# Two selective scans: the rounding helper of softplus moves from ScalarE to GpSimd, scan inputs are shared out anew, and the preparation of the next chunk is reordered

## The reference, cut to what matters

```python
# layer 1 (first scan): 128 channels d, 64 states n, positions l = 4096 in each of 4 images
u = layernorm(x @ W_in[:, :128]) * gamma + beta
dt, B_ssm, C_ssm = split(u @ W_dt + b_dt, [8, 64, 64])
delta = softplus(dt @ W_dtr + b_dtr)
h[l] = exp(delta[l] * A) * h[l-1] + delta[l] * B_ssm[l] * u[l]      # for each d, n
y = sum_n(h * C_ssm) + u * D + xc * silu(xc)                        # xc: 3x3 depthwise convolution
out = x + y @ W_out
# layer 3 (second scan): the same recurrence with 256 channels, 16 states, over all 16384
# positions, once forwards and once backwards; both results are added and group-normalised
```

## Time and profile before

| | us |
|---|---|
| median of 3 runs | 10018.97 (10010.94 to 10019.53) |
| the profiled execution, its time | 10018.13 |
| the profiled execution, its span | 10016.3 |
| busy in the span: PE, DVE, ACT, POOL | 9175.6, 7849.4, 7926.6, 5764.0 |
| first scan's scans, from the first to the end of the last | 2837.3 to 5734.1 |
| second scan's scans | 6802.0 to 9929.3 |

### The profile page before, as it was taken

How to read it: one execution, slowest core, us unless ns; L and a number is a source line. 1 busy time by engine, 2 the same in 40 slices (tenths; PEclk the granted TensorE clock), 3 DMA queues, 4 the chain that set the end, 5 groups by cost and what they waited for, 6 DMA issues and landing times. The chain is left out here.

```text
span 10016.3 us, 147659 instructions
## 1 busy us (share of the span) xinstructions
PE 9175.6 (92%) x51972; PEld 4789.2 (48%) x51972; DVE 7849.4 (78%) x5926; ACT 7926.6 (79%) x14573; POOL 5764.0 (58%) x3092
## 2 busy tenths in 40 slices
PE   9999999999978888888888899998999999999995
PEld 6767767767733333333333344443333333333332
DVE  7858858858669999999999911117999999999997
ACT  5646646646578998999989855559999999999996
POOL 0000000000068998999989800008999999999996
PEclk9999999999989999999999999999999999999998
DMA  0000000000045555556556500005666666666666
GB/s 40 0 1 0 0 1 0 0 1 0 0 135 185 193 193 183 191 189 195 190 185 194 177 8 8 8 20 171 206 209 203 211 205 211 211 208 212 206 209 232
DMA packets 338546, 1249.85 MB, mean 125 GB/s; under 512 B 39280, under 2 KB 39408, under 8 KB 334448
## 3 DMA queue, kind: packets, MB, share of 16 engines
q1 hardware_dynamic: 338032, 1243.13, 38.2%
HBM read 1144.41 MB, written 56.62 MB: 120 GB/s over the span
## 5 line engine op out<-in xcount | busy, mean ns | idle before, releaser
L2066 DVE TENSOR_TENSOR_SCAN l_h<-l_ring,l_h,l_ps 128x1024 f32<-128x1024 f32 x960 | 2201.5, 2334 | 112.4 <-PE l_ps L1626 87.2
L1024 POOL TENSOR_TENSOR l_hc<-l_h,l_hc 128x1024 f32<-128x1024 f32 x1024 | 2027.0, 2000 | 223.6 <-DVE l_h L1131 201.1
L1989 POOL TENSOR_TENSOR l_ring<-l_h,l_ring 128x1024 f32<-128x1024 f32 x1024 | 2026.3, 2002 | 136.3 <-DVE l_h L2066 130.6
L1131 DVE TENSOR_TENSOR_SCAN l_h<-l_decay,l_h,l_ps 128x1024 f32<-128x1024 f32 x768 | 1747.7, 2330 | 82.1 <-PE l_ps L717 76.0
L117 POOL COPY l_qm<-l_q 128x128 f32 x128 | 82.9, 650 | 2576.2 <-PE l_ps L189 2180.1
L900 ACT ACTIVATE l_xt<-l_duT,l_BT 128x128 f32<-128x128 f32 x4224 | 1286.6, 389 | 113.7 <-PE l_ps L717 112.7
L1856 ACT ACTIVATE l_xt<-l_duT,l_BT 128x128 f32<-128x128 f32 x3840 | 1171.4, 393 | 16.4 <-PE l_ps L1626 15.2
L1643 PE MATMUL l_ps<-l_ring,w_sb 64*64 64x512 f32 x8192 | 1135.4, 625 | 2.5 <-ACT l_gate L1780 1.2
L734 PE MATMUL l_ps<-l_hc,w_sb 64*64 64x512 f32 x8192 | 1137.0, 626 | 0.7 <-POOL l_hc L1024 0.3
L213 PE MATMUL l_ps<-l_attnT,l_vT 128*128 128x128 f32 x8192 | 1096.3, 277 | 1.3 <-ACT l_attnT L284 1.3
L213 PEld LDWEIGHTS l_ps<-l_attnT,l_vT 128*128 128x128 f32 x8192 | 1014.6, 192 | 138.1 <-issue 114.7
(11 more groups left out here) (238 smaller groups left out, 14929.0 us busy)
## 6 DMA issues: line engine op xcount, KB each, us to landing
l_hc<-l_rows_dram SPq DMA_DIRECT2D x1024, 512.0 KB, 4.8
l_ring<-l_rows_dram SPq DMA_DIRECT2D x1024, 512.0 KB, 5.1
l_crossed<-l_delta SPq DMA_DIRECT2D x160, 256.0 KB, 3.5
l_gate_dram<-l_gate SPq DMA_DIRECT2D x32, 512.0 KB, 6.7
l_recon_dram<-l_recon SPq DMA_DIRECT2D x32, 512.0 KB, 6.6
l_gate<-l_gate_dram SPq DMA_DIRECT2D x32, 512.0 KB, 5.6
l_xw<-x_dram SPq DMA_DIRECT2D x30, 513.5 KB, 6.9
x_dram<-x SPq DMA_DIRECT2D x16, 512.0 KB, 2.6
```

The source lines that it names most:

```text
L1024: nc.gpsimd.tensor_tensor(hc[:, unit % CS, :], h[:, unit % HS, window(unit)][:, along(K)], hc[:, unit % CS, :], ALU.mult).then_inc(hc_done, 1)
L1131: nc.vector.tensor_tensor_scan(h[:, unit % HS, window(unit)][:, along(K)], decay[:, unit % DS, :], odd_in if odd else even_in, before, ALU ...
L1989: nc.gpsimd.tensor_tensor(hc[:, unit % CS, :], h[:, unit % HS, window(unit)][:, along], hc[:, unit % CS, :], ALU.mult).then_inc(hc_done, 1)
L2066: nc.vector.tensor_tensor_scan(h[:, unit % HS, window(unit)][:, into], decay[:, unit % DS, order], x_now[:, order], before, ALU.mult, ALU. ...
```

## The change

`z + 1 - 1` is formed on GpSimd by one tensor_scalar (add 1, add -1) in `soft_low`, with a semaphore of its own before the subtraction that reads it; ScalarE's two Identity instructions and the constant `minus_one` go. In the first scan `MADE` grows from 13 to 15 pairs, `TURNED` stays at 14 with other members, `crossed` gets a second buffer, and the preparation is moved by about two pairs on every engine. In the second scan pair 2 leaves `MADE3` (its odd input is turned by ScalarE), and pair 6 forwards and pair 3 backwards leave `TURNED3` (even inputs by VectorE). `rest` starts two columns (8 bytes) further in both scans.

```diff
-TURNED = (1, 2, 3, 5, 7, 9, 11, 13, 20, 23, 24, 28, 29, 31)
-MADE = (0, 1, 3, 5, 9, 11, 12, 17, 19, 20, 24, 29, 30)
+TURNED = (2, 3, 5, 7, 9, 11, 15, 18, 20, 23, 24, 28, 30, 31)
+MADE = (1, 2, 3, 5, 9, 13, 14, 15, 17, 19, 20, 22, 23, 29, 31)
...
-        crossed = sb("crossed", [128, CH])
+        crossed = sb("crossed", [128, 2, CH])
-        rest = sb("rest", [DT_AT + R1, CH])
+        rest = sb("rest", [DT_AT + R1, CH + 4])[:, 2:CH + 2]
...
@@ sync, first scan @@
-                at_least(sp, decay_ready, S1 * K)
+                at_least(sp, decay_ready, S1 * (K - 1))
-                    if q == 30 and K + 1 < NCH:
+                    if q == 34 and K + 1 < NCH:
                         store_rows(K + 1)
-                    if q == 62 and K + 1 < NCH:
+                    if q == 56 and K + 1 < NCH:
                         cross_delta(K + 1)
@@ tensor, first scan @@
-            CONV = {3: (0, 0), 7: (0, 1), **{14 + i: (0, 2 + i) for i in range(7)}, **{23 + i: (1, i) for i in range(9)}}
+            CONV = {k: (i // 9, i % 9) for i, k in enumerate((3, 5, 6, 8, 9, 11, 12, 13, 14, 20, 22, 23, 24, 25, 26, 28, 30, 31))}
-                        if k in (1, 2):
-                            prep_u(K + 1, k - 1)
-                        if k == 5:
+                        if k in (1, 4):
+                            prep_u(K + 1, k // 4)
+                        if k == 7:
                             prep_var(K + 1)
...
-                        if k in (25, 27):
-                            prep_duT(K + 1, 1 - p, (k - 25) // 2)
+                        if k in (27, 29):
+                            prep_duT(K + 1, 1 - p, (k - 27) // 2)
@@ scalar, both scans @@
             def soft_log(K):
-                act.wait_ge(exp_ln, 3 * K + 1)
-                nc.scalar.activation(z3[:], z1[:], ACT.Identity, bias=1.0)
-                act.drain()
-                nc.scalar.activation(z3[:], z3[:], ACT.Identity, bias=wt("minus_one")).then_inc(exp_ln, 1)
+                act.wait_ge(exp_ln, 2 * K + 1)
                 act.wait_ge(stack_ready, K + 1)
                 nc.scalar.activation(z2[:], z1[:], ACT.Ln, bias=1.0).then_inc(exp_ln, 1)
-                    if k == 21:
+                    if k == 16:
                         silu(K, 0)
-                        if k in (2, 3):
-                            u_copy(K + 1, 1 - p, k - 2)
+                        if k in (3, 4):
+                            u_copy(K + 1, 1 - p, k - 3)
...
@@ gpsimd, both scans @@
             def soft_low(K):
-                pool.wait_ge(exp_ln, 3 * K + 2)
+                pool.wait_ge(exp_ln, 2 * K + 1)
+                nc.gpsimd.tensor_scalar(z3[:], z1[:], 1.0, -1.0, ALU.add, ALU.add).then_inc(rounded, 1)
+                pool.wait_ge(rounded, K + 1)
                 nc.gpsimd.tensor_tensor(z3[:], z1[:], z3[:], ALU.subtract).then_inc(low_ready, 1)
@@ gpsimd, first scan: squares 3 -> 5, newton 7 -> 9, split_rest 14 -> 16, split_last 16 -> 18,
@@ soft_low 20 -> 22, soft_max 21 -> 23, soft_sum 22 -> 24, input_rate 23 -> 25
@@ vector, first scan: gate_conv(K, 0) 21 -> 17, rstds 5 -> 7, scale_u 8, 9 -> 10, 11, bt_copy 15 -> 17
...
-TURNED3 = {True: (6,), False: (3, 6)}
-MADE3 = {True: (2, 6), False: (2, 6)}
+TURNED3 = {True: (), False: (6,)}
+MADE3 = {True: (6,), False: (6,)}
```

More of the change, by code:

```diff
@@ L529, in scan_layer @@
         c_in = [sem(f"c_in_{i}") for i in range(CS)]
-        crossed_in = sem("crossed_in"); first_half_mm = sem("first_half_mm")
+        crossed_in = [sem(f"crossed_in_{i}") for i in range(2)]; first_half_mm = sem("first_half_mm")
         hc_done = sem("hc_done"); sum_mm = sem("sum_mm"); y_out = sem("y_out"); yg_ready = sem("yg_ready")
@@ L578, in cross_delta @@
                 sp.wait_ge(delta_ready, K + 1)
-                at_least(sp, decay_ready, S1 * K)
+                at_least(sp, decay_ready, S1 * (K - 1))
                 for side in range(2):
-                    sp.dma_start(crossed[64 * side:64 * side + 64, :],
-                                 delta[64 - 64 * side:128 - 64 * side, K % 2, :]).then_inc(crossed_in, 16)
+                    sp.dma_start(crossed[64 * side:64 * side + 64, K % 2, :],
+                                 delta[64 - 64 * side:128 - 64 * side, K % 2, :]).then_inc(crossed_in[K % 2], 16)
             sp.dma_start(conv_raw, conv_weights).then_inc(conv_in, 16)
@@ L881, in decays @@
                 if q == 1:
-                    act.wait_ge(crossed_in, 32 * K + 32)
+                    act.wait_ge(crossed_in[K % 2], 32 * (K // 2) + 32)
                 at_least(act, scan_done, unit - DS + 1)
-                nc.scalar.activation(decay[:, unit % DS, :], crossed[:] if q % 2 else delta[:, p, :], ACT.Exp,
+                nc.scalar.activation(decay[:, unit % DS, :], crossed[:, p, :] if q % 2 else delta[:, p, :], ACT.Exp,
                                      scale=wt("A")[:, q:q + 1]).then_inc(decay_ready, 1)
@@ L1054, in _ @@
                         odd_input(P + 1, p if k + 1 < PAIRS else 1 - p)
-                    if K + 1 < NCH and k == 7:
+                    if K + 1 < NCH and k == 9:
                         newton(K + 1)
@@ L1156, in _ @@
                     scan(P, 1)
-                    if k == 1 and K:
-                        add_y(K - 1, 1 - p)
                     if P + 1 < NCH * PAIRS and k + 1 not in TURNED:
@@ L1161, in _ @@
                     if k == 1 and K:
+                        add_y(K - 1, 1 - p)
+                    if k == 1 and K:
                         gate_conv(K - 1, 1)
-                    if k == 21:
+                    if k == 17:
                         gate_conv(K, 0)
@@ L1391, in two_way_scan_layer @@
         yg = sb("yg", [128, 3, CH + 4])[:, :, 2:CH + 2]
-        rest = sb("rest", [128, CH])
+        rest = sb("rest", [128, CH + 4])[:, 2:CH + 2]
         part = sb("part", [PARTS * SEL, CH], BF16)
@@ L1942, in soft_low @@
                 def soft_low(T):
-                    pool.wait_ge(exp_ln, 3 * T + 2)
+                    pool.wait_ge(exp_ln, 2 * T + 1)
+                    nc.gpsimd.tensor_scalar(z3[:], z1[:], 1.0, -1.0, ALU.add, ALU.add).then_inc(rounded, 1)
+                    pool.wait_ge(rounded, T + 1)
                     nc.gpsimd.tensor_tensor(z3[:], z1[:], z3[:], ALU.subtract).then_inc(low_ready, 1)
                 def soft_max(T):
-                    pool.wait_ge(exp_ln, 3 * T + 3)
+                    pool.wait_ge(exp_ln, 2 * T + 2)
                     nc.gpsimd.tensor_tensor(delta[:, T % 2, :], delta[:, T % 2, :], z2[:], ALU.add).then_inc(max_ready, 1)
@@ L2260, in layer1_arrays @@
                ("A", 0, _np.where(_np.arange(S1) % 2, _np.roll(A_log[:, by_unit], 64, 0), A_log[:, by_unit])),
[L2261 removed]
+               ("below_top", 0, below_top),
                ("bdt_b", 0, column(_np.concatenate([b_dt[even_B]] * PARTS + [b_dt[:R1]]))),
```

82 lines of the change are left out of this document (39 added, 43 removed).

## The result

| | time, us | scan 1 | scan 2 |
|---|---|---|---|
| before | 10019.25 (10010.94 to 10023.13) | 2896.9 | 3127.2 |
| after | 10295.81 (10288.78 to 10305.88) | 2822.0 | 3468.9 |

The ratio is 1.0281, interval [1.0268, 1.0294]. The first scan gained 74.9 us, where the prediction had 95. The second lost 341.7, where it had 142. So the sign was right and the size far off: 10060 was forecast, and the time lies beyond the range's end of 10120.

What follows compares the result with a forecast made beforehand. The second scan was taken as bound by a chain from pair 2's first scan through GpSimd and TensorE to unit 13. 10018 + 142 (second scan) - 95 (first scan) = 10065, stated as 10060 us; range 9975 to 10120.

Steps and rivals of the forecast that it cites:

- The price of the two-scalar instruction: GpSimd, pair 2 of the second scan: the add-and-add tensor_scalar on 1024 columns takes 1.1 us, bounds 0.9 and 2.0.
- The chain: Second scan, pair 2's first scan through GpSimd and TensorE to unit 13: 25.5 us grows by 1.3, 82 us over 63 stages.
- The 0.2 us for the semaphore: GpSimd's subtraction in the second scan now waits for a semaphore, adding 0.2 us to each stage.
- The clock: Second scan, forward stages: TensorE's longer wait lowers its clock, 2.2 us a stage, 60 us net; nothing backwards.
- The first scan: New order removes waits at `prep_u`, `add_y` and `prep_var`, 9.1 us a stage; with GpSimd's lag, -95 us in all.
- The lag of a full GpSimd: First scan: GpSimd, as full as VectorE, falls behind and TensorE waits three times; 2.8 us a stage, between 0.5 and 6.
- `add_y`'s wait: First scan: VectorE's 2.3 us a stage, laid to a sum behind pair 2's transposes, falls to 0.4.
- That the chain is not the bound: Rival: ScalarE sets the second scan's pace, so relieving it gains 1 us a stage, 64; 9865 to 9925 us; chance 0.08.
- That the instruction costs 2.0: Rival: the scalar instruction takes 2.0 us, adding 57 us in the second scan and 10 in the first; 10125; chance 0.10.
- That GpSimd's load eats the first scan's gain: Rival: GpSimd's lag in the first scan costs 6 us a stage instead of 2.8; 10105 us; chance 0.12.
- That the clock stays up: Rival: TensorE's longer forward wait lowers its clock no oftener, so the second scan costs 82; 9990 us; chance 0.20.
- VectorE's extra even input: Second scan: one more a stage, 1.21 us, falls into VectorE's wait before unit 13 and costs nothing.

Runs made afterwards that it cites:

- copy_for_rounding: The changed kernel with a plain GpSimd copy in place of the two-scalar instruction in both scans: 10040.59 us, ratio 1.0026 to the kernel before.
- copy_filled: copy_for_rounding plus 24 extra transposes before TensorE's wait for the odd input of pair 6 in the second scan: 9935.45 us, ratio 0.9922.
- filled_wait: The changed kernel plus 36 extra transposes before TensorE's wait for the odd input of pair 6 in the second scan: 10191.64 us, ratio 1.0177.
- first_scan_alone: The kernel before with only the first scan's new order and lists; rounding on ScalarE, second scan's shares as before: 9879.30 us, ratio 0.9866.
- the best kernel: The changed kernel with rounding back on ScalarE in both scans, plus 12 extra transposes before TensorE's second-scan wait: 9863.35 us, ratio 0.9850.
- the price kernel: The kernel before plus seven GpSimd instructions, four times each, on scratch tiles between the two scans, to time them alone: 10018.6 us.

## Why the prediction was off

**The price of the two-scalar instruction** is the step that failed. I had "I take 1.1", from two rows on eight columns, with bounds of 0.9 and 2.0. It is 3.63, far beyond the upper one. The eight-column rows are nearly all fixed cost, and I took another instruction's fixed part, 189 ns, for this one's. Nine ns were left for eight columns, where eight at 3.3 ns would be 26: a few ns more or less in the fixed part decide the price of 1024 columns. (The straight line through the larger sizes would give some 245 ns at eight columns, for the 198 of the row, whose operations are a multiplication and an addition. So that line doesn't reach so far down either.) And the upper bound, "no cheaper than two inputs", was a guess about how the engine works and not a row. copy_for_rounding shows that this step carried nearly all of the miss: with 1.04 the forecast would have been 20 us too high instead of 236 too low. That it would have been so close is in part luck. At that price the chain grows by 63 x 1.04 = 66 us for the 82 taken, the clock costs some 80 for the 60 taken, and these two errors cancel.

**The chain** was right. It starts with pair 2's first scan, ends at unit 13, and hands on what is put in: 1.04 gave 26.54, 3.63 gave 29.16. The 0.2 us for the semaphore were too many: from the tensor_scalar to the subtraction that waits for it there are 3.71 us in the changed kernel (7829.50 to 7833.21), and 3.59 to the next instruction where nothing is waited for (7752.77 to 7756.36), so 0.12. In the changed kernel the chain's growth is 63 x 3.66 = 231 us, where I had 82.

**The clock** was right as a mechanism and too narrow. I gave it to the forward stages alone and nothing backwards, "TensorE's wait stays as it is". That was wrong even at the forecast price: in copy_for_rounding the next pair is late in 31 of 32 forward and 30 of 31 backward stages. My argument was that backwards both the chain and VectorE move by 1.2 us; but unit 13 has to wait for TensorE's transposes, and TensorE's wait grew there too, from 2.1 to 3.2 us in the mean. Worked out from copy_filled, in which the median next pair takes 3.69 us: forwards the clock costs (0.47 + 1.52) x 32 = 64, backwards (0.83 + 0.75) x 31 = 49 us (mean delay of unit 13, then of the next pair), 113 together for the 107 measured. Before already paid some 32 of this: its next pairs come after 3.98 us forwards and 4.26 backwards in the mean, 0.29 x 32 + 0.57 x 31, and unit 13 0.08 late. Forwards 12 of these 32 go off, which leaves 52, about the 60 taken; backwards it leaves some 30 that weren't in the sum. In the changed kernel the same sum, with filled_wait's 29.16 for unit 13, is (0.94 + 1.35) x 32 + (0.94 + 1.44) x 31 = 147, 115 net. With 231 from the chain it makes 346, for 341.7 measured. The split is an estimate: filled_wait itself got 94 of the 147 back.

**The first scan** was right in its gain: 9.1 us a stage forecast, (2896.9 - 2753.1) / 15 = 9.6 measured. The lag of a full GpSimd was right in kind. At a price of 1.04 it costs (2778.7 - 2752.5) / 15 = 1.7 us a stage, at 3.63 it is (2822.0 - 2752.5) / 15 = 4.6, for the 2.8 taken. The waits in the profile after (us, times, longest) and stage 6 on TensorE:

```profile
DVE l_h L1130 <- PE l_ps L717: 64.7, 27, 4.2
...
PE l_ps L663 <- POOL l_du L1012: 59.5, 15, 4.0
...
DVE l_h L1130 <- POOL l_hc L1023: 15.4, 45, 1.7
```

```profile
4048.16 1.12 PE L663 MATMUL l_ps<-w_sb,l_du 128*128 128x128 f32 x4 [3.97 <-POOL l_du L1012]
```

It is one long wait a stage, for `du` before the first `prep_duT`, and not three of 1.5 to 2.7 us. VectorE stands up to 4.2 us before the next scan. I had put `add_y`'s wait down to TensorE being late at pair 2, and so to the order; it was mostly the lists that removed it.

**The rivals.** That the chain is not the bound: out; unit 13 moved with the chain in each run. That the instruction costs 2.0: the right direction, and far too little. That GpSimd's load eats the first scan's gain, 6 us a stage: 4.6, between it and the forecast. That the clock stays up: out; in the changed kernel it fell, and in copy_for_rounding too. copy_filled keeps it up by force and its second scan is 38 us longer than before's, where that rival had 82: some 16 of the 44 us between are the price and the semaphore (63 x 0.26), and the rest is about the 32 that before lost to the clock and the extra transposes gave back. VectorE's extra even input costs nothing, as forecast: it is busier (64 instructions more, 76.9 us) and first_scan_alone is no faster.

## What to carry to other kernels

An instruction that isn't in the trace has no price until one of its kind and size is measured; a row on few columns gives only the fixed part, and a bound from a neighbour of another kind is no bound. Then ask where it stands: in a chain that starts and ends in the engine that sets the pace it came out whole in every stage, and TensorE's lower clock behind the longer wait added half as much again; a pair earlier, partly in GpSimd's idle time, 1.1 of its 3.6 us came out, and the clock's share beside them. Where TensorE must wait for another engine in every stage, work that is thrown away can be worth its place: 12 small transposes a stage gave 21 us in the best kernel, 24 gave 107 in one with a longer wait. Which waits are worth filling is read from the stages in which something behind them comes late.

## What the hardware showed

- On GpSimd, 1024 fp32 columns took 1.04 us in a copy, 1.89 in a tensor_tensor, 2.77 in a tensor_scalar with one operation and 3.63 with two. The first one of the price kernel took 5.55 us, its three repeats 3.63.
- Two columns' shift of `rest` made GpSimd's subtractions on it faster. One row of the price kernel, in which `rest` lies as before, and one of the changed kernel (shapes apart, and one line):

```profile
L1964 POOL TENSOR_TENSOR l_rest<-l_rest,l_part 96x1024 f32<-96x1024 f32 x32 | 68.3, 2134 | 966.3 <-DMA l_rows_dram<-l_rest 966.3
```

```profile
L1932 POOL TENSOR_TENSOR l_rest<-l_rest,l_part x32: 1988/1993/2002, 6704.1 to 10054.5; 96x1024 f32<-96x1024 f32 x32
```

  2134 ns against 1993; why the offset matters is not settled here, since output and inputs moved against each other as well as `rest` itself.
- The granted clock had fallen behind TensorE's waits of 3.6 and 6.2 us, and with the 3.6 filled to 0.7 us it had not: 0.95 over the second scan of copy_for_rounding, 0.99 in copy_filled.

```profile
6679.00:9952.00 3273.00, 2914.27 (x16082) 1207.78 (x16082) 3015.38 (x1658) 2956.37 (x5896) 2938.50 (x1528) 0.95 0.60 198
```

```profile
6678.00:9843.00 3165.00, 2978.77 (x17614) 1290.00 (x17618) 3014.25 (x1656) 2949.87 (x5895) 2931.04 (x1527) 0.99 0.63 205
```
